# Building the edge-count matrix: comparisons in 16-bit neighbours, an earlier product, and waits bank by bank

## What is computed

```python
edge_index = jnp.stack([src, dst])
h = jnp.maximum(_layernorm(x), 0.0);  x = x + L0(h, edge_index)      # ten steps of normalised propagation
h = jnp.maximum(_layernorm(x), 0.0);  x = x + L1(h, W, att, bias)    # graph attention, softmax over in-edges
h = jnp.maximum(_layernorm(x), 0.0);  x = x + L2(h, qW, kW, vW)      # dot-product attention, four heads
h = jnp.maximum(_layernorm(x), 0.0);  x = x + L3(h, edge_index, W, b) # mean of messages over in-edges
```

## Time and profile before

| | us |
|---|---|
| median of 3 executions (1594.42 to 1600.21) | 1600.06 |
| the profiled execution | 1606.92 |
| its span | 1605.1 |
| first instruction of the four layers | 315.50 |
| VectorE busy | 1260.8 |
| TensorE busy | 1244.5 |
| ScalarE busy | 519.1 |
| GpSimd busy | 346.3 |

### The profile page before, as it was taken

One profiled execution on the slowest core, in us unless ns is written; L12 is line 12 of the kernel. 1 busy time (PEld: TensorE's weight loads), 2 busy tenths in 40 slices (PEclk: granted clock), 3 DMA queues, 4 the chain that ended last, 5 costly groups with the idle time before them and its releaser, 6 DMA issues. The chain is left out here.

```text
span 1605.1 us, 44909 instructions
## 1 busy us (share of the span) xinstructions
PE 1244.5 (78%) x18543; PEld 1185.8 (74%) x18544; DVE 1260.8 (79%) x2327; ACT 519.1 (32%) x1021; POOL 346.3 (22%) x211
## 2 busy tenths in 40 slices
PE   4757877589899899899898400688884899999378
PEld 4356766489899899899898300677774799999378
DVE  7888888667677577577565899899998799999732
ACT  0047776500000000000000587233333677777310
POOL 1400000000000000000000101488884355556200
PEclk6867777689999999999999655899998899999679
DMA  0012322377766586578540476455553367777393
GB/s 11 0 47 100 110 99 109 117 237 285 270 243 245 221 293 231 220 265 298 194 155 2 145 223 242 165 207 201 192 187 116 115 248 279 278 263 254 122 330 95
DMA packets 88810, 297.51 MB, mean 185 GB/s; under 512 B 22399, under 2 KB 23976, under 8 KB 88604
## 3 DMA queue, kind: packets, MB, share of 16 engines
q1 hardware_dynamic: 66668, 231.86, 40.7%
q10 hardware_dynamic: 21600, 61.45, 9.9%
q0 software_dynamic: 336, 1.20, 0.3%
HBM read 188.31 MB, written 106.16 MB: 183 GB/s over the span
## 5 line engine op out<-in xcount | busy, mean ns | idle before, releaser
L1298 PE MATMUL psum<-work,count 128*128 128x192 f16 x6250 | 527.9, 249 | 39.4 <-issue 39.4
L1298 PEld LDWEIGHTS psum<-work,count 128*128 128x128 f16 x6250 | 525.5, 99 | 41.8 <-issue 40.5
L1639 PE MATMUL psum<-count 128*128 128x98 f16 x625 | 113.2, 209 | 134.5 <-DVE count L1686 98.2
L935 ACT ACTIVATE work<-work 128x1248 f32<-128x1248 f32 (+1 forms) x6 | 7.2, 1203 | 591.7 <-DVE work L918 591.6
L1678 POOL TENSOR_TENSOR count<-count 128x970 bf16<-128x970 f32 (+1 forms) x75 | 166.6, 2235 | 91.4 <-ACT count L1671 91.4
L1904 PE MATMUL psum<-count 128*128 128x100 f16 (+1 forms) x1875 | 176.7, 207 | 10.6 <-DVE count L1988 6.6
L1217 DVE SCALAR_TENSOR_TENSOR work<-psum,small,work 128x96 f32<-128x96 f32 x250 | 79.2, 317 | 133.1 <-PE psum L1298 132.7
L1905 PE MATMUL psum<-count 128*128 128x100 f16 (+1 forms) x1875 | 176.6, 207 | 0.0
L1904 PEld LDWEIGHTS psum<-count 128*128 128x128 f16 x1875 | 162.6, 98 | 14.7 <-DVE count L1988 10.7
L1639 PEld LDWEIGHTS psum<-count 128*128 128x128 f16 x625 | 61.1, 98 | 141.1 <-DVE count L1686 98.3
L1905 PEld LDWEIGHTS psum<-count 128*128 128x128 f16 x1875 | 164.1, 98 | 1.3 <-issue 1.3
(11 more groups left out here) (286 smaller groups left out, 2689.0 us busy)
## 6 DMA issues: line engine op xcount, KB each, us to landing
count<-onehots_by_src SPq DMA_DIRECT2D x75, 800.0 KB, 7.0
count<-bucket_rows_by_dst SPq DMA_DIRECT2D x50, 800.0 KB, 4.3
x<-bucket_rows_by_src SPq DMA_DIRECT2D x75, 400.0 KB, 6.3
onehots_by_src<-x ACTq DMA_DIRECT2D x75, 400.0 KB, 6.1
count_f<-count SPq DMA_DIRECT2D x25, 800.0 KB, 7.6
count<-count_turned SPq DMA_DIRECT2D x25, 800.0 KB, 5.2
count<-count_f SPq DMA_DIRECT2D x17, 800.0 KB, 4.3
count_turned<-x SPq DMA_DIRECT2D x25, 416.0 KB, 2.4
```

Of the source, the lines that this page charges most:

```text
L1298: last = nc.tensor.matmul(bank[i % BANKS], count16[:, j, i * P:(i + 1) * P], y[par][:, j, :], start=(j == 0), stop=(j == TILES - 1))
L1639: nc.tensor.matmul(ps[:, at:at + GW], node_hot[SRC][t % 2][:, s, :], high[:, s, :], start=True, stop=False, skip_group_check=True)
```

## The change

**Comparisons in 16-bit neighbours.** `src_hot` is laid out `[tile][block]`. It is made from `src_hi_16` and `tile_pairs`, both fp16, in a pattern whose innermost step is a pair of neighbours. `local_ids` and `id_rows` are laid out with the block (or window column) innermost, so that line 596's product reads and writes neighbours too. TensorE now reads a window column of `id_rows` in steps of 20 elements, and the histogram's loads are neighbours. `b_lo` is rounded down to an even block by three more linked instructions, so that a window starts at an even column.

**Ends ahead of the prefix.** VectorE counts `prep` up before it waits for the histogram, and TensorE has the end products (line 225) ahead of the prefix products (line 220).

**Ranking in pairs.** Four banks instead of two (`rank_bank`: 0, 1 and 5, 6), TensorE waits only from the fifth chunk on, and VectorE takes two chunks in one product and one sum of 800 elements. The sum reads its 25 terms 16 elements (64 bytes) apart.

**Waits bank by bank.** Batch 0 waits only for batch 2 of the tile before, batch 1 for batch 3. The degree products move from ahead of batch 0 to behind batch 1, with a semaphore of their own (`degree_made`) that VectorE waits for ahead of line 645. ScalarE copies batch 2 after five groups instead of seven.

```diff
-    src_hot = work.take(NB * TILES, F16).rearrange("p (b t) -> p b t", t=TILES)
+    src_hot = work.take(NB * TILES, F16).rearrange("p (t b) -> p t b", b=NB)
-    local_ids = work.take(2 * NB, F16).rearrange("p (b v) -> p b v", v=2)
+    local_ids = work.take(2 * NB, F16).rearrange("p (v b) -> p v b", v=2)
-    id_rows = work.take(WINDOW * 2 * TILES, F16).rearrange("p (u v s) -> p u v s", u=WINDOW, v=2)
+    id_rows = work.take(WINDOW * 2 * TILES, F16).rearrange("p (v s u) -> p v s u", u=WINDOW, v=2)
...
-            nc.vector.tensor_tensor(src_hot, iota_t.unsqueeze(1).broadcast_to([P, NB, TILES]),
-                                    src_hi_f[:, 0:NB].unsqueeze(2).broadcast_to([P, NB, TILES]), ALU.is_equal).then_inc(hist_hot, 1)
+            in_two = [P, TILES, NB // 2, 2]
+            nc.vector.tensor_tensor(src_hot.rearrange("p s (b d) -> p s b d", d=2), tile_pairs.unsqueeze(2).broadcast_to(in_two),
+                                    src_hi_16[:, 0:NB].rearrange("p (b d) -> p b d", d=2).unsqueeze(1).broadcast_to(in_two), ALU.is_equal).then_inc(hist_hot, 1)
...
+            link(nc.vector.tensor_copy(cols_i[0:32, 2:3], b_lo))
+            link(nc.vector.tensor_scalar(cols_i[0:32, 2:3], cols_i[0:32, 2:3], -2, None, ALU.bitwise_and))
+            link(nc.vector.tensor_copy(b_lo, cols_i[0:32, 2:3]))
...
+            dve.sem_inc(prep, 1)
             dve.wait_ge(totals_done, 1)
             for c in range(4):
                 n = min(P, NB - c * P)
                 link(nc.vector.tensor_copy(totals[0:n, c, :], bank(4)[0:n, c * TILES:(c + 1) * TILES]))
-            dve.sem_inc(prep, 1)
             dve.sem_inc(prep, 1)
...
-            for i, (b0, n) in enumerate(RCH):
-                dve.wait_ge(prefixed, i + 1)
-                prod = picked[:, 0:n * TILES].rearrange("p (b s) -> p b s", s=TILES)
-                nc.vector.tensor_tensor(prod, src_hot[:, b0:b0 + n, :], bank(i % 2, n * TILES).rearrange("p (b s) -> p b s", s=TILES), ALU.mult).then_inc(ranked, 1)
-                dve.wait_ge(ranked, i + 1)
-                link(nc.vector.tensor_reduce(rank[:, b0:b0 + n], prod, AX.X, ALU.add))
+            for k, i in enumerate(range(0, len(RCH), 2)):
+                c, b0 = min(2, len(RCH) - i), RCH[i][0]
+                dve.wait_ge(prefixed, i + c)
+                prod = picked[:, 0:c * RB * TILES].rearrange("p (c s b) -> p c s b", c=c, s=TILES)
+                hots = src_hot[:, :, b0:b0 + c * RB].rearrange("p s (c b) -> p c s b", c=c)
+                counts = rank_bank(i, c) if c > 1 else rank_bank(i).unsqueeze(1)
+                nc.vector.tensor_tensor(prod, hots, counts, ALU.mult).then_inc(ranked, 1)
+                dve.wait_ge(ranked, k + 1)
+                link(nc.vector.tensor_reduce(rank[:, b0:b0 + c * RB].rearrange("p (c b) -> p c b", c=c), prod.rearrange("p c s b -> p c b s"), AX.X, ALU.add))
...
                 if b == 0:
+                    pe.wait_ge(copied, act_copied_after(t - 1, 2))
+                elif b == 1:
                     pe.wait_ge(copied, act_copied_after(t - 1, 3))
...
-                    nc.vector.tensor_tensor(id_rows, tiles_hot.unsqueeze(2).broadcast_to([P, WINDOW, 2, TILES]),
-                                            local_ids[:, bass.ds(at, WINDOW), :].unsqueeze(3).broadcast_to([P, WINDOW, 2, TILES]), ALU.mult)
+                    nc.vector.tensor_tensor(id_rows, tiles_hot.unsqueeze(1).broadcast_to([P, 2, TILES, WINDOW]),
+                                            local_ids[:, :, bass.ds(at, WINDOW)].unsqueeze(2).broadcast_to([P, 2, TILES, WINDOW]), ALU.mult)
...
                         dve.wait_ge(turned, turned_after(t, 0))
+                        dve.wait_ge(degree_made, t)
```

69 lines of the change are left out of this document (42 added, 27 removed).

## The result

| | before | after |
|---|---|---|
| median | 1600.13 us (4 runs, 1594.42 to 1607.03) | 1576.13 us (4 runs, 1575.27 to 1578.25) |
| the profiled execution | 1606.92 | 1575.27 |
| its span | 1605.1 | 1573.4 |
| first instruction of the four layers | 315.50 | 287.88 |
| ranking, first product to last sum | 32.93 | 35.78 |

The ratio is 0.985, with a 95% interval of 0.981 to 0.989. A second comparison gave 1572.63 us against 1600.37, ratio 0.982 (0.980 to 0.985). The forecast was 1573.8 us, range 1566 to 1589. The total fits, and luck has a part in it: two of its four larger terms fit, two others missed by 6.5 and 4.5 us in opposite directions, and the tail gave 2.8 us that weren't in the sum.

What follows compares the result with a forecast made beforehand. The build was taken as bound by its preparation and ranking chain, then two nearly equal tile-loop circles (VectorE; ScalarE with TensorE). Terms -5.4 + 0.5 - 5.2 - 3.6 - 12.6 = -26.3 us gave 1580.6 profiled, median 1573.8, range 1566 to 1589 us.

Steps and rivals of the forecast that it cites:

- bucket comparison: Preparation: with 16-bit neighbours VectorE's comparison of 10300 elements falls from 10.89 to 5.47 us, saving 5.42.
- rounding: Preparation: three linked instructions that round the first block to even, starting 0.18 us apart, add 0.54 us.
- ends ahead of the prefix, with GpSimd's contention: Preparation: picks and prefix run side by side, 5.9 us earlier; GpSimd's spot products beside later steps cost 0.7; net -5.2.
- ranking in pairs: Ranking: pairs take 2.05 us against 2.42, first pair waits 0.9 us for its second chunk; net -3.6 us.
- tile loop: Loop over 25 tiles: 8.4 to 7.9 us in 23 steps, plus 1.05 us for two tiles ahead; -12.6 us.
- tail: Behind the tile loop: moves as a whole; new turning order worth at most 1 us either way, counted as 0.
- rival of a second tick: Ranking's sum: 64-byte steps cost a second tick per element, +10.4 us, giving 1584.2 us; chance 0.18 alone.
- as the sequencer's fixed loop cost, not as a wait for TensorE: Tile loop: the 1.32 us from copy start to next taking was counted in VectorE's own 8.35 us per tile.
- each edit alone would have left the other circle: Tile loop: two chains repeating each tile, VectorE's and ScalarE-TensorE's; shortening only one leaves 8.35 to 8.4 us.
- The placing's columns: Tile loop: TensorE's id products read columns 40 bytes apart, costing between nothing and 0.8 us a tile.
- rival of TensorE as the bound: Tile loop: strided columns and low clock make TensorE's serial order fill 8.2 to 8.4 us; about 1583 us; chance 0.13 alone.
- the prediction's last sentence: Layers behind 315.5 us: if their length changes, the forecast fails; 1 in 100 of their 1290 us is half the gain.

## Why the prediction was right, and where it was not

Term by term, in us, from the two profiles:

| step | forecast | measured |
|---|---|---|
| bucket comparison | -5.4 | -5.4 |
| rounding | +0.5 | +0.5 |
| ends ahead of the prefix, with GpSimd's contention | -5.2 | -5.6 |
| ranking in pairs | -3.6 | +2.9 |
| tile loop | -12.6 | -17.1 |
| tail | 0 | -2.8 |
| sum | -26.3 | -27.5 |
| start of the layers | | -27.6 |

The forecast's 12.6 for the loop holds 1.05 us for two id products ahead of it; the measured 17.1 goes from the first taking to the last, and ahead of it 0.25 us came between the ranking and the first taking. The bucket comparison started 0.2 us later than before. With these two the stages add up to the start of the layers.

**The preparation** went as worked out. The ends' move gave 5.93 us against 5.9. The contention with GpSimd was 0.3 us, not 0.7: from the products behind the picks to the first ranking product it is 6.41 us instead of 6.09. All of it is in one instruction, VectorE's product of 625 elements, which takes 1.11 us beside the spot products and took 0.80 without them. The spot product beside it takes 1.43 us; the other three take 0.86 to 0.87, as all four did before, so their new layout isn't the reason.

**The ranking** is the term that was mis-sized. The product took the forecast 0.99 us, the second chunk's wait 0.86 (0.9), TensorE and GpSimd stayed hidden. The sum took 1.51 us and not 0.99: 0.52 x 12.5 = 6.5 us, all of the miss. The prediction had two ends, 0.99 and 1.82, and took the lower, with the words "that row is on another engine". The rival of a second tick (+10.4) named the right mechanism with too high a price; the measured price is six tenths of it. The earlier trace rows were the nearest rows and showed a cost, and the rule of the Trainium skill (Advanced Engine Details and Errata, section SBUF Cachelines), as the prediction cites it, said that there would be one. The right choice was a value between the ends, not the end without a row.

**The loop** had the right sign for a wrong reason. The step that failed is the reading of the gap ahead of the taking "as the sequencer's fixed loop cost, not as a wait for TensorE". Its argument was that the gap is nearly the same in both tiles of the earlier trace rows. It is the same because the whole circle repeats. The earlier trace rows name TensorE as releaser ahead of 172.09; the profile's "issue" ahead of 180.44 is the same wait, met earlier. VectorE waits for TensorE ahead of its degree sum. That wait costs no idle time at the degree sum itself when it is met while VectorE still works. Its sequencer, though, comes to the end of the loop's turn only 0.15 us behind the event, and needs another 1.48 to 1.50 us for the next tile's numbers. So the prediction was right that the sequencer has a fixed piece of work there, and wrong that the tile must pay for it. With the waits alone, where the degree products end 1.83 us ahead of the taking at 180.11, the gap is gone. A row that contradicts the reading stands in the trace of the kernel before:

```profile
230.74 0.26 DVE L618 TENSOR_SCALAR x<-psum 128x100 f16<-128x100 f32 x1 [0.69 <-issue]
...
237.77 0.62 DVE L646 COPY x<-psum 128x896 f16<-128x896 f16 x1
238.70 0.26 DVE L618 TENSOR_SCALAR x<-psum 128x100 f16<-128x100 f32 x1 [0.31 <-issue]
```

This tile takes 7.96 us with the same work. A fixed cost can't be 0.69 in one tile and 0.31 in the next. The distance from the degree products, on the other hand, is 1.96 and 1.95 us in these two. So "each edit alone would have left the other circle" was wrong too: the waits alone gave the loop 19.1 us.

**The placing's columns** were rightly seen and priced too low: between nothing and 0.8 us a tile, measured 1.14. The rival of TensorE as the bound was right in part of its mechanism, since the slow placing holds the degree products and with them every taking back; but TensorE isn't busy throughout, it has 3.60 of the circle's 7.45 us. Of the 1.14 us, 0.38 reach the degree products (3.60 against 3.22 us from the first placing product with neighbours), mostly because the quick placing must wait for VectorE's second half. It was wrong in its time, 8.2 to 8.4 us a tile, because the tile without them would be 7.2 us and not 7.8. Two errors met: the free circle is shorter than forecast, and the columns cost more, and 7.65 came out where 7.9 was forecast.

**The tail** had been given 0 with "1 us either way". The gain stands from its first round on: ScalarE's first copy comes 4.08 us after the last taking instead of 7.86, and its last copies 15.67 instead of 18.79.

**The layers** are the part that no step touches, and the prediction's last sentence was right to fear them: 8 us between two profiles of the same program. The step from the profiled execution to the median went wrong by them. The profiled execution was forecast at 1580.6 us and took 1575.27, with 1.3 us of the difference from the build and 4.1 from shorter layers. The 6.9 us that the prediction took off for the median didn't come again: the median lies 0.9 us above the profiled execution. These errors cancelled as well, and the total came out 2.3 us from the forecast by luck as much as by the terms.

## What to carry to other kernels

A gap that has the same length in every pass of a loop is not shown to be a fixed cost; measure its distance from the event on the other engine, over all passes, and look for the one pass where it differs. A wait that costs nothing where it stands can cost at the next instruction that needs values from the sequencer. And where a layout is changed for one engine, price the reader on the other: two neighbours on a line were enough here for both, in the ranking (6.5 us) and in the placing (7.1 us, with the slower id product paid).

## What the runs showed of the hardware

- VectorE pays for a step of 16 bytes and more, and not for one of 8: 1.49 to 1.75 us instead of 0.99 for sums of 800 elements, 1.79 for a product of 800 written in 100-byte steps, 1.01 to 1.07 instead of 0.69 for products of 512, read or written. Pairs of fp32 neighbours with a jump behind each are free in this slow form (0.99).
- In the fast form of 16-bit operands, a jump behind each pair in the output is not free: 500 elements take 0.60 us, while 1000 elements with neighbours take 0.68.
- TensorE reads 50 columns 40 bytes apart at 1.0 us for ten products instead of 0.43; 4 bytes apart they cost next to nothing (186 ns against 184 in the median). Steps between the two were not tried.
- An odd start of the fp16 operand makes the product of 1000 elements 732 ns instead of 680.
- A wait holds VectorE's sequencer too: behind the degree sum's wait, its work for the next turn of the loop starts 0.15 us after the last degree product and the taking comes 1.48 to 1.50 us after that (22 of 22 tiles of the changed kernel; 1.47 to 1.50 us in the two profiles of the kernel before). The profile shows it as idle time ahead of the taking, marked "issue" or with TensorE as releaser, not at the wait. Where the wait is met early enough, nothing of it shows.
- Beside GpSimd's products, VectorE's small instructions get longer: a comparison of 0.24 us took 0.90, a product of 0.80 us took 1.11, and the GpSimd product beside the latter 1.43 us instead of 0.86.
